# Centring the first two token tiles ahead of their roots in a gated two-layer kernel

## The chip, the core and the metric

The kernel runs on one NeuronCore of a Trainium2 chip. The metric is the device time of one execution in microseconds (us): the median of three runs, and beside it one execution under the hardware profiler, from which the rows come. TensorE multiplies matrices, VectorE and ScalarE work element by element, GpSimd issues the gathers and scatters of rows, SyncE (SP) issues the plain transfers.

## The reference

There are 2048 tokens of width 512. Two layers follow one another, each added to its input through a gate:

```
x = x + tanh(g_xattn) * experts_by_token_id(layernorm(x))     # 4 experts
x = x + tanh(g_ffn) * (top-2 of 16 experts + shared MLP)(layernorm(x))
```

In the first layer expert `e` uses one 512x512 matrix, its context `C`, for all three products: `y = (silu(h C^T) * (h C^T)) C^T`, where `h` is the normalised token `(x - mean) / sqrt(var + 1e-5)` and the expert follows from the token's id (ids of 18750 and more all go to the last of the four). The second layer routes each token to two of sixteen small gated MLPs, 256 places each, and adds a shared MLP. The change lies in the first layer alone.

## The kernel before

**Precision.** Products run in TensorE's fp32r form on operands split in two: a high part (the value rounded) and a low part (what is left). A product of two split operands is three matmuls: high by high, high by low, low by high (`product`, L1291). For a context the high part is a ScalarE copy (`high_ctx`, L562). The low part comes in one of two ways: VectorE subtracts (`low_ctx`, L834), or TensorE forms `ctx - high` with the identity and its negative (`rest`, L1320 and L1321) and ScalarE copies it out of PSUM (`take_rest`, L571).

**The opening.** VectorE sorts the tokens by expert into tiles of 128 rows, 19 places for tiles in all. GpSimd gathers the rows of the tiles (`gather_xa`, L433). SP loads the four contexts of 1 MB; the last of them goes out when the rows of tile 2 have landed, and four writes of zeros to spare rows of the output (256 KB each) follow it. The input gives tile 0 to expert 0, tile 1 to expert 1, tiles 2 and 3 to expert 2, the rest to expert 3. TensorE may begin the product of a tile of expert `w` once `ctx_lo_done` is above `w`.

**Stage 1.** Each engine runs its own `step(t)` for t from -2 to 20, and the order within a step is written out by hand. In step `t` the engines work on several tiles at once:

- for tile t+2: VectorE takes statistics (`bn_stats` L943, `bn_aggr` L961) and finds one over the root with ten small instructions on a column per tile (L976 to L993; "root" below); ScalarE applies scale and bias (`norm`, L583) into `h`;
- for tile t+1: TensorE transposes `h` (L1296), ScalarE copies the high part (`hT`, L608), VectorE subtracts for the low part (`low_h`, L925);
- for tile t: TensorE forms the product with the context into `psG`, ScalarE takes silu (L605), VectorE multiplies (`gate1`, L932) into `gu`;
- for tile t-1: TensorE transposes `gu`, high and low parts follow (L589, `low_g` L921), and the second product goes into `psY`;
- for tile t-2: VectorE adds the result to x (L916), takes statistics (L950) and the root together with tile t+2; ScalarE normalises for the second layer (L583), SP writes these rows to `padded` (L380) and GpSimd scatters x and h to the output buffer (L445).

The buffers of `h`, `hT`, `gT`, `gu` and `psY` are few, so the steps are tied by semaphores. VectorE, ScalarE and TensorE take their instructions strictly in program order. In ScalarE's step 1 the high part of context 3 stands ahead of silu:

```
if known == 1:
    high_ctx(3)
...
if have(known, 0):
    act.wait_ge(p_ps, t + 1)
    ...
    act.activation(s_sb[:, 0:D], psG[0][:, :], ACT.Silu).then_inc(s_ready, 1)
```

In the opening of before, tile 0 has its own root; tiles 1 and 2 share one ("pair"). Context 1's low part is one VectorE pass of 2048 columns, context 2's comes from four `rest` products, context 3's from two VectorE passes of 1024 columns in steps 1 and 2. SP's loop over tiles also sends the slices of the shared MLP's weights: two of 192 KB for each of the tiles 1 to 4, one for each of the tiles 5 to 8.

Of the kernel before, what the change touches and what calls it, by code (L numbers as in the profile page):

```python
# [31 lines left out]
P = 128  # L32
# [46 lines left out]
def gated_layer(nc, x, ids, ctx_t, gates, w13, w2, gate_b, const, out):  # L79
    stack = ExitStack()  # L80
    with stack:  # L81
# [91 lines left out]
        stats = sb("stats", [P, 2, 6])  # L173
        mv = sb("mv", [P, 2, 2])
        nwt = sb("nwt", [P, 5, 2])
# [57 lines left out]
        ctx_hi_done, ctx_lo_done = sem("ctx_hi_done"), sem("ctx_lo_done")  # L233
# [95 lines left out]

        def ctx_raw(e):  # L330
# [23 lines left out]
        def _(sp):  # L354
# [20 lines left out]
            sp.wait_ge(zeroed, 1)  # L375
            for a, b in ((a, b) for a in range(NA) for b in range(2)):
                sp.dma_start(out[TOK + a * P:TOK + (a + 1) * P, b * D:(b + 1) * D], zeros[:, :]).then_inc(spare_sent, 16)
            for t in range(NT):
# [5 lines left out]
                if 1 <= t <= 4:  # L384

                    for n in range(2):
                        load_slice((t - 1) // 2, 2 * ((t - 1) % 2) + n)
                elif 5 <= t <= 8:

                    load_slice(2, t - 5)  # L390

# [22 lines left out]
        def _(pool):  # L414
# [133 lines left out]
        def _(act):  # L548
# [15 lines left out]
            def take_rest(e, i):  # L564

                act.wait_ge(rest_ps, e // 2 * KD + i + 1)
                if e and i == KD - 1:

                    act.wait_ge(ctx_lo_done, 2)
# [8 lines left out]
            high_ctx(2)  # L578
# [7 lines left out]
            def step(t, par, known):  # L586
# [14 lines left out]
                if have(known, 0):  # L601
# [3 lines left out]
                    act.activation(s_sb[:, 0:D], psG[0][:, :], ACT.Silu).then_inc(s_ready, 1)  # L605
# [8 lines left out]
                act.wait_ge(norm_ready, t + 3)  # L614
                if have(known, 2):
                    if had(known, 1):
                        act.wait_ge(hT_ps, t + 1)
                    norm(h[:, par, :], xa_of(t, par, known), 1 if known == 0 else 0, h_ready)
                if known == FIRST:
                    take_rest(2, 0)  # L620
# [180 lines left out]
        def _(dve):  # L801
# [76 lines left out]
            for j in range(NJ):  # L878
# [17 lines left out]
                                     ALU.is_ge, ALU.add).then_inc(tile_ready, 1)  # L896
            dve.wait_ge(tg_ready, 1)
# [10 lines left out]
            def step(t, par, known):  # L908
                one, two = have(known, 2) and known != 0, have(known, -2)
# [18 lines left out]
                def gate1():  # L928
# [3 lines left out]
                    dve.tensor_tensor(gu[:, 0:D], s_sb[:, 0:D], psG[0][:, :], ALU.mult).then_inc(gu_ready, 1)  # L932

                if known == 0:
                    gate1()
                    low_h()

                pair = known == FIRST + 1
                cs = slice(0 if one else 1, 2 if two or pair else 1)
# [4 lines left out]
                low_g()  # L944
                if pair:
                    xa_landed(dve, 0, 0, 0)
                    i = dve.bn_stats(stats[:, 1, :], xa_of(0, 0, 0))
# [3 lines left out]
                k = t + 2  # L951
                if one or two:
# [4 lines left out]
                if one or two:  # L957
                    dve.wait_ge(stats_done, NORMS(k, known))
# [3 lines left out]
                    if two or pair:  # L962
                        i = dve.bn_aggr(mv[:, 1, :], stats[:, 1, :])
                    i.then_inc(mv_done, 1)
                    dve.wait_ge(mv_done, NORMS(k, known))
                    base = (NORMS(k, known) - 1) * NEWTON
# [12 lines left out]
                    for m in range(2):  # L979
                        nw(dve.tensor_tensor(T, V, Y, ALU.mult))  # L980
                        nw(dve.tensor_tensor(T, T, Y, ALU.mult))
                        if m == 0:
                            nw(dve.scalar_tensor_tensor(Y, T, -((27 / 4 * RS_W) ** (1 / 3)), Y, ALU.add, ALU.mult))
                            if pair:
                                low_h()
                    nw(dve.scalar_tensor_tensor(T, T, -10 / 3 * RS_W, T, ALU.add, ALU.mult))
                    if had(known, 2):
                        dve.wait_ge(h_ready, t + 2)
# [652 lines left out]
```

## Time and profile before

| quantity | value |
|---|---|
| median of 3 runs | 479.32 us (479.09 to 480.01) |
| profiled execution | 480.27 us, of which the span of instructions is 478.5 us |
| TensorE busy | 460.1 us, 96% of the span |
| VectorE busy | 328.6 us, 69% |
| ScalarE busy | 255.4 us, 53% |
| GpSimd busy | 211.1 us, 44% |
| mean granted clock of TensorE | 0.995 |

TensorE's share is an average over the whole run. In the first 5 us it does nothing; from 10 us on it is busy nearly throughout. Stage 1 ends near 160 us; behind it come the second layer's shared MLP, the routing and the sixteen experts.

### The profile page before, as it was taken

How to read it: one execution, taken by the hardware profiler on the slowest of the kernel's cores; microseconds unless marked ns; L12 is line 12 of the kernel's file. 1: busy time of each engine (PE TensorE's matmuls, PEld its weight loads, DVE VectorE, ACT ScalarE, POOL GpSimd, SP SyncE). 2: the span in 40 equal slices, each digit the busy share in tenths (PEclk: the TensorE clock that was granted, in tenths of full speed). 3: DMA queues.
4: the chain of work that ended last, by engine and by line, in shares of the span. 5: the costliest groups of instructions: out<-in, count | busy, mean ns of one | idle time of the engine just before them, and what ended most of it. 6: DMA issues, size and time to landing. Idle time of an engine off the chain costs nothing.

```text
span 478.5 us, 7813 instructions
## 1 busy us (share of the span) xinstructions
PE 460.1 (96%) x2493; PEld 392.7 (82%) x2493; DVE 328.6 (69%) x724; ACT 255.4 (53%) x379; POOL 211.1 (44%) x175
## 2 busy tenths in 40 slices
PE   2999999999999999999999999999999999999993
PEld 1477778888888888888888999999999999999992
DVE  6689899998987844488559776676666666667520
ACT  4764445545553543542436575656655676666531
POOL 0513444565443475435177445434525545542242
PEclk9999999999999999999999999999999999999998
DMA  7643656876665443363379999989869998887555
GB/s 298 187 174 125 198 179 201 292 258 226 206 214 175 175 121 114 86 79 46 43 198 185 296 294 264 267 279 272 266 193 263 254 267 269 264 248 226 110 63 70
DMA packets 30460, 95.02 MB, mean 199 GB/s; under 512 B 4960, under 2 KB 7008, under 8 KB 29920
## 3 DMA queue, kind: packets, MB, share of 16 engines
q0 software_dynamic: 17040, 43.66, 37.3%
q1 hardware_dynamic: 13104, 50.98, 31.2%
q8 instruction: 17, 0.28, 0.2%
q14 instruction: 11, 0.09, 0.1%
q10 hardware_dynamic: 288, 0.01, 0.0%
HBM read 67.50 MB, written 28.70 MB: 201 GB/s over the span
## 4 chain that ended last, share of the span: by engine, by line
PE 91%; DVE 3%; DMA 2%; ACT 1%; issue 1%; POOL 0%; POOLq 0%; DVEq 0%
PE psG L1291 49%; PE psY L1291 30%; PE psT L1296 7%; PE psG L1549 1%; DMA out<-xh_sb,idx 1%; PE psG L1320 1%; DMA tok_i<-in_ids 1%; PE psY L1308 1%; ACT arena L571 0%; POOLq L81 0%; ACT arena L562 0%; PE psY L1427 0%; PE psG L1321 0%; POOL out L521 0%; ACT front L583 0%
## 5 line engine op out<-in xcount | busy, mean ns | idle before, releaser
L1291 PE MATMUL psY<-arena 128*128 (+1 forms) x372 | 91.0, 394 | 0.4 <-DVE arena L921 0.4
L1291 PEld LDWEIGHTS psY<-arena 128*128 128x128 f32 x372 | 68.8, 188 | 14.8 <-issue 0.8
L512 POOL DMA_INDIRECT ht<-out,idx x32 | 33.6, 1051 | 64.6 <-PE psT L1296 48.8
L1291 PE MATMUL psY<-slot,arena 128*128 128x512 f32 x240 | 59.0, 395 | 0.0
L1066 DVE TENSOR_TENSOR slot<-raw,slot 128x1536 fp32r<-128x1536 f32 x25 | 43.9, 1760 | 19.7 <-ACT slot L638 19.6
L1291 PE MATMUL psG<-arena 128*128 x228 | 57.0, 398 | 0.0
L1066 DVE TENSOR_TENSOR arena<-raw,arena 128x1536 fp32r<-128x1536 f32 x24 | 42.0, 1756 | 16.6 <-ACT arena L638 16.4
L1291 PEld LDWEIGHTS psY<-slot,arena 128*128 128x128 f32 x240 | 44.2, 188 | 9.5 <-ACT xh_sb L682 0.3
L1291 PE MATMUL psG<-arena,slot 128*128 128x512 f32 x216 | 51.3, 392 | 0.0
L1291 PEld LDWEIGHTS psG<-arena 128*128 128x128 f32 x228 | 41.5, 188 | 8.5 <-issue 0.4
L1291 PEld LDWEIGHTS psG<-arena,slot 128*128 128x128 f32 x216 | 40.1, 188 | 8.2
L753 ACT ACTIVATE s_sb<-psG 128x224 f32<-128x224 f32 (+1 forms) x48 | 17.5, 365 | 54.8 <-PE psG L1291 54.8
L521 POOL DMA_INDIRECT out<-ys,idx x16 | 31.7, 1980 | 31.2 <-ACT ys L742 22.4
L521 POOL DMA_INDIRECT out<-xb,idx x16 | 29.7, 1853 | 33.3 <-ACT xb L742 23.1
L1291 PE MATMUL psG<-bl,slot 128*128 128x256 f32 (+1 forms) x264 | 42.1, 314 | 0.0
L1291 PE MATMUL psG<-slot,bl 128*128 128x448 f32 x192 | 40.3, 365 | 0.0
L1291 PE MATMUL psG<-arena,bl 128*128 128x448 f32 x192 | 40.3, 365 | 0.0
L1291 PEld LDWEIGHTS psG<-bl,slot 128*128 128x128 f32 x264 | 37.3, 189 | 3.0
L433 POOL DMA_INDIRECT front<-in_x,idx x17 | 17.0, 999 | 51.3 <-ACT front L583 39.9
L498 POOL DMA_INDIRECT out<-xh_sb,idxc x16 | 27.8, 1738 | 26.5 <-ACT xh_sb L682 24.6
L1291 PEld LDWEIGHTS psG<-slot,bl 128*128 128x128 f32 x192 | 36.0, 188 | 3.4
L1291 PEld LDWEIGHTS psG<-arena,bl 128*128 128x128 f32 x192 | 36.0, 188 | 3.3
(228 smaller groups left out, 803.9 us busy)
## 6 DMA issues: line engine op xcount, KB each, us to landing
raw<-in_w SPq DMA_DIRECT2D x48, 768.0 KB, 5.6
padded<-xh_sb SPq DMA_DIRECT2D x19, 256.0 KB, 2.2
raw<-in_w SPq DMA_DIRECT2D x12, 192.0 KB, 4.3
raw<-in_ctx_t SPq DMA_DIRECT2D x2, 1024.0 KB, 8.7
ht<-in_ctx_t SPq DMA_DIRECT2D x1, 1024.0 KB, 11.7
xh_sb<-in_ctx_t SPq DMA_DIRECT2D x1, 1024.0 KB, 9.5
out<-log_sb SPq DMA_DIRECT2D x4, 256.0 KB, 8.2
ht<-out,idx POOLq DMA_INDIRECT x32, 4.5
```

Of the source, the lines that this page charges most:

```text
L433: pool.indirect_dma_start(buf, None, x, rows_of(t, 0)).then_inc(xa_here[t if t < 4 else t % 2], 16)
L498: pool.indirect_dma_start(halves_of_out, ranked(1, j), y2[j % 4], None, compute_op=ALU.add).then_inc(y2_sent[j % 4], 16)
L512: pool.indirect_dma_start(ht[:, n, :], None, halves_of_out, slots(e * NA + a, 0)).then_inc(g_here[n], 16)
L521: pool.indirect_dma_start(halves_of_out, slots(e * NA + a, 1), y3[e % 2][:, a, :], None, compute_op=ALU.add).then_inc(added[a], 16)
L753: act.activation(dst, src, ACT.Silu).then_inc(silu3, 1)
L1066: dve.tensor_tensor(piece(SLOT[r][1], c), raw[:, c, :], as_f32(piece(SLOT[r][0], c)), ALU.subtract).then_inc(w_lo[c], 1)
L1291: ins = pe.matmul(ps, left[a], right[b], start=n == 0 and m == 0, stop=n == total - 1 and m == 2)
L1296: ins = pe.transpose(ps[:, k * P:(k + 1) * P], src[:, k * P:(k + 1) * P], ident)
L1308: ins = pe.matmul(psY[1][:, 0:2 * NT], onehot1[:, j, :], q_tok[0][:, j, 0:2 * NT], start=j == 0, stop=j == NJ - 1)
L1320: pe.matmul(psG[i][:, :], ident, ctx_raw(e)[:, s], start=True, stop=False)
L1549: ins = pe.transpose(psG[3][:, o:o + P], gu[:, s:s + P], ident)
```

## The change

Tiles 0 and 1 are no longer normalised before their first product, only centred: VectorE subtracts the mean of tile 0, ScalarE that of tile 1. The factor one over the root is applied behind the product, as the scale of silu and as a factor in the gate. One root then serves tiles 0, 1 and 2. Context 1's low part is half a VectorE pass (after GpSimd's first two gathers, `first_out`) and half two `rest` products; context 2's is two VectorE passes, in steps 0 and 1. In step 1 VectorE does the gate and the low part of h before the next tile's statistics and root. Tile 0's first product runs in three passes, one for each pair of parts, with a wait ahead of each. The zeros of the spare rows are written behind tiles 9 to 12. The core of the diff:

```diff
 SP
-            sp.wait_ge(zeroed, 1)
-            for a, b in ((a, b) for a in range(NA) for b in range(2)):
-                sp.dma_start(out[TOK + a * P:..., b * D:(b + 1) * D], zeros[:, :])...
             for t in range(NT):
...
+                elif 9 <= t <= 12:
+                    if t == 9:
+                        sp.wait_ge(zeroed, 1)
+                    a, b = divmod(t - 9, 2)
+                    sp.dma_start(out[TOK + a * P:..., b * D:(b + 1) * D], zeros[:, :])...
 GpSimd
             gather_xa(0)
+            gather_xa(1)
             pool.memset(cur[:, :], 0).then_inc(first_out, 1)
-            for t in range(1, 4):
+            for t in range(2, 4):
                 gather_xa(t)
 ScalarE
             take_rest(0, 0)
             take_rest(0, 1)
-            high_ctx(2)
             take_rest(0, 2)
             take_rest(0, 3)
...
+                    if known in CENTERED:                      # CENTERED = (0, 1)
+                        act.wait_ge(norm_ready, 1)
+                        act.activation(s_sb[:, 0:D], psG[0][:, :], ACT.Silu,
+                                       scale=nwt[:, 3, known:known + 1]).then_inc(s_ready, 1)
...
                 if known == -1:
-                    take_rest(2, 1)
-                    take_rest(2, 2)
+                    act.wait_ge(mean1_ready, 1)
+                    act.activation(h[:, 1, :], xa[:, 1, :], ACT.Identity, bias=nwt[:, 4, 1:2]).then_inc(h_ready, 1)
+                    take_rest(1, 2)
+                    high_ctx(2)
                 if known == 0:
-                    take_rest(2, 3)
+                    take_rest(1, 3)
...
-                if known == FIRST:
-                    take_rest(2, 0)
 VectorE
+            dve.wait_ge(first_out, 1)
+            low_ctx(1, 0, 2).then_inc(ctx1_half, 1)
...
+                    if known in CENTERED:
+                        dve.scalar_tensor_tensor(gu[:, 0:D], psG[0][:, :], nwt[:, 3, known:known + 1], s_sb[:, 0:D],
+                                                 ALU.mult, ALU.mult).then_inc(gu_ready, 1)
...
+                if known == FIRST:
+                    mean_of(0)
+                    dve.tensor_scalar(h[:, 0, :], xa[:, 0, :], mv[:, 0, 0:1], None, ALU.subtract).then_inc(h_ready, 1)
+                    mean_of(1)
+                    dve.tensor_scalar(nwt[:, 4, 1:2], mv[:, 1, 0:1], -1.0, None, ALU.mult).then_inc(mean1_ready, 1)
                 if known == 0:
                     gate1()
                     low_h()
+                    link(low_ctx(2, 0, 2))
+                if known == 1:
+                    low_g()
+                    dve.wait_ge(ctx_lo_done, 2)
+                    low_ctx(2, 1, 2).then_inc(ctx_lo_done, 1)
+                    gate1()
+                    low_h()
...
+                third = known == FIRST + 1
+                if third:
+                    low_h()
+                cs = slice(0 if one or third else 1, 3 if third else 2 if two else 1)
...
-                if have(known, 0) and known != 0:
+                if have(known, 0) and known > 1:
                     gate1()
-                if have(known, 1) and known not in (FIRST + 1, 0):
+                if have(known, 1) and known > 1:
                     low_h()
-                if pair:
-                    dve.wait_ge(ctx_lo_done, 1)
-                    low_ctx(1, 0, 1).then_inc(ctx_lo_done, 1)
 TensorE
             for i in range(KD):
                 rest(0, i)
-            rest(2, 0)
-            pe.wait_ge(rest_taken, KD)
+            pe.wait_ge(rest_taken, 1)
...
+                if known == 0:
+                    for m, (a, b) in enumerate(((0, 0), (0, 1), (1, 0))):
+                        pe.wait_ge(*((hT_hi, 1), (ctx_lo_done, 1), (hT_lo, 1))[m])
+                        for k in range(KD):
+                            ins = pe.matmul(psG[0][:, :], hT[a][:, k * P:(k + 1) * P], ctx(0, k)[b],
+                                            start=m == 0 and k == 0, stop=m == 2 and k == KD - 1)
+                    ins.then_inc(p_ps, 1)
...
                 if known == -1:
-                    rest(2, 1)
-                    rest(2, 2)
+                    rest(1, 2)
                 if known == 0:
-                    rest(2, 3)
+                    rest(1, 3)
```

`mean_of(k)` waits for the rows of tile k and takes `bn_stats` and `bn_aggr` of them, with its own waits on VectorE between the two.

## Rows read from the trace of the kernel before

**Rows 1.** The chain that ended last, opening and stage 1 (start us, us, what).

```profile
20.80 0.63 PE psT L1296 x4
...
49.37 6.94 DMA out<-xh_sb,idx
...
62.46 1.23 PE psT L1296 x8
```

**Rows 2.** TensorE's waits, whole run (us in total, times, longest us).

```profile
PE psT L1296 <- DVE gu L932: 1.1, 2, 0.8
```

**Rows 3.** Timeline of VectorE (start us, us; idle before and releaser in brackets).

```profile
16.16 0.69 DVE L943 BATCH_NORM_STATS2 stats<-front 128x6 f32<-128x512 f32 x1 [2.65 <-DMA front<-in_x,idx]
...
17.17 0.15 DVE L976 TENSOR_SCALAR nwt<-mv 128x1 f32<-128x1 f32 x1
...
23.72 2.29 DVE L834 TENSOR_TENSOR arena<-raw,arena 128x2048 fp32r<-128x2048 f32 x1
...
29.75 0.69 DVE L921 TENSOR_TENSOR arena<-psT,arena 128x512 fp32r<-128x512 f32 x1 [0.83 <-ACT arena L589]
...
30.57 0.15 DVE L976 TENSOR_SCALAR nwt<-mv 128x1 f32<-128x1 f32 x1
...
32.38 0.69 DVE L932 TENSOR_TENSOR gu<-s_sb,psG 128x512 f32<-128x512 f32 x1
32.99 0.68 DVE L925 TENSOR_TENSOR arena<-psT,arena 128x512 fp32r<-128x512 f32 x1
33.59 1.21 DVE L834 TENSOR_TENSOR arena<-xh_sb,arena 128x1024 fp32r<-128x1024 f32 x1
34.84 0.75 DVE L916 SCALAR_TENSOR_TENSOR xh_sb<-psY,tg,xb 128x512 f32<-128x512 f32 x1
35.50 0.68 DVE L943 BATCH_NORM_STATS2 stats<-front 128x6 f32<-128x512 f32 x1
...
40.83 1.25 DVE L834 TENSOR_TENSOR arena<-xh_sb,arena 128x1024 fp32r<-128x1024 f32 x1
...
56.51 0.75 DVE L916 SCALAR_TENSOR_TENSOR xh_sb<-psY,tg,xb 128x512 f32<-128x512 f32 x1 [1.15 <-DMA out<-xh_sb,idx]
```

**Rows 4.** Timeline of GpSimd, the opening.

```profile
15.19 0.95 POOL L433 DMA_INDIRECT ys<-in_x,idx  x1 [0.30 <-issue]
...
25.20 1.62 POOL L433 DMA_INDIRECT front<-in_x,idx  x1 [3.83 <-ACT front L583]
...
40.82 0.94 POOL L433 DMA_INDIRECT front<-in_x,idx  x1 [4.02 <-ACT front L583]
```

**Rows 5.** Timeline of ScalarE, the opening.

```profile
19.34 0.82 ACT L583 ACTIVATE front<-front,nwt 128x512 f32<-128x512 f32 x1
...
29.61 1.91 ACT L562 ACTIVATE arena<-xh_sb 128x2048 fp32r<-128x2048 f32 x1
31.49 0.60 ACT L605 ACTIVATE s_sb<-psG 128x512 f32<-128x512 f32 x1
```

**Rows 6.** Timeline of TensorE, the opening.

```profile
17.86 0.79 PE L1321 MATMUL psG<-arena,minus 128*128 128x512 f32 x1
...
22.35 1.02 PE L1320 MATMUL psG<-ht,cst 128*128 128x512 f32 x2
...
23.44 2.93 PE L1291 MATMUL psG<-arena 128*128 x12
...
28.46 2.99 PE L1291 MATMUL psG<-arena 128*128 x12
```

**Rows 7.** Timeline of SP's queue, the opening (start us, us of issue).

```profile
18.95 0.33 SPq L373 DMA_DIRECT2D xh_sb<-in_ctx_t  x1
```

**Rows 8.** DMA issues of 18.85 to 20 us (KB each, us from issue to landing).

```profile
xh_sb<-in_ctx_t SPq DMA_DIRECT2D x1, 1024.0 KB, 9.5
```

**Rows 9.** DMA packets by size, of 22 to 23 us and of 27 to 28 us.

```profile
DMA packets 33, 0.26 MB, mean 262 GB/s; under 512 B 1, under 2 KB 1, under 8 KB 1
...
DMA packets 204, 0.39 MB, mean 391 GB/s; under 512 B 34, under 2 KB 34, under 8 KB 201
```

More of the change, by code:

```diff
@@ L390, in _ @@
                     load_slice(2, t - 5)
+                elif 9 <= t <= 12:
+                    if t == 9:
+                        sp.wait_ge(zeroed, 1)
+                    a, b = divmod(t - 9, 2)
+                    sp.dma_start(out[TOK + a * P:TOK + (a + 1) * P, b * D:(b + 1) * D], zeros[:, :]).then_inc(spare_sent, 16)
             sp.wait_ge(bT_ps, NJ)
@@ L908, in step @@
             def step(t, par, known):
-                one, two = have(known, 2) and known != 0, have(known, -2)
+                one, two = have(known, 2) and known > 0, have(known, -2)
                 if two:
@@ L950, in step @@
                     i = dve.bn_stats(stats[:, 1, :], xh_sb[:, par, 0:D])
-                k = t + 2
-                if one or two:
+                groups = t + 3 if known >= 1 else 3
+                base = NEWTON * max(t, 0)
+                if one or two or third:
                     i.then_inc(stats_done, 1)
@@ L956, in step @@
                     transposed(TB + 1)
-                if one or two:
-                    dve.wait_ge(stats_done, NORMS(k, known))
+                if one or two or third:
+                    dve.wait_ge(stats_done, groups)
                     dve.nop(nofuse=True)
@@ L961, in step @@
                         i = dve.bn_aggr(mv[:, 0, :], stats[:, 0, :])
-                    if two or pair:
+                    if two:
                         i = dve.bn_aggr(mv[:, 1, :], stats[:, 1, :])
+                    if third:
+                        i = dve.bn_aggr(mv[:, 2, :], stats[:, 2, :])
                     i.then_inc(mv_done, 1)
-                    dve.wait_ge(mv_done, NORMS(k, known))
-                    base = (NORMS(k, known) - 1) * NEWTON
+                    dve.wait_ge(mv_done, groups)
                     n = [0]
@@ L983, in step @@
                             nw(dve.scalar_tensor_tensor(Y, T, -((27 / 4 * RS_W) ** (1 / 3)), Y, ALU.add, ALU.mult))
-                            if pair:
-                                low_h()
                     nw(dve.scalar_tensor_tensor(T, T, -10 / 3 * RS_W, T, ALU.add, ALU.mult))
-                    if had(known, 2):
-                        dve.wait_ge(h_ready, t + 2)
+                    if third or one:
+                        dve.wait_ge(h_ready, t + 2 if one else 2)
                     if had(known, -2):
@@ L1058, in rank_tokens @@
                 dve.tensor_copy(idxc[:, 2, :], S(31)).then_inc(rank_idx, 1)
-            def NORMS(k, known):
-                return (1, 2, None, 3)[k] if known is not None and known < 2 else k
             def split(s, c, r):
@@ L1346, in step @@
             def step(t, par, known):
-                if have(known, 0):
+                if have(known, 0) and known > 0:
                     w = weights(t)
@@ L1365, in step @@
                     half_up(0, 1)
-                if have(known, 0):
+                if known == 0:
[5 more added lines that the diff above has]
+                    ins.then_inc(p_ps, 1)
+                elif have(known, 0):
                     pe.wait_ge(hT_lo, t + 1)
```

49 lines of the change are left out of this document (29 added, 20 removed).

## The prediction

> **What bounds the kernel now.** I read the chain that ended last first. In the opening it runs over all engines, and the first transposes of a token tile stand at 20.80 us; from 62.46 us on it is TensorE alone [rows 1]. So whatever the change wins must reach 62.46. Between the two the chain runs through VectorE and, at 49.37, through a 6.94 us scatter of finished rows. TensorE's waits say the same: for gates it waited twice, 1.1 us in all [rows 2]. So VectorE's timeline came next [rows 3]. From 29.75 us it works without a gap to 55.36, where it waits 1.15 for that scatter: statistics, the small root instructions, gate, low parts, in program order. The landmark is L916 at 34.84, which adds the first finished tile to x; I call it X0. From X0 to the scatter and on to 62.46 each step hangs on VectorE's order, which the change leaves alone there. A shift of X0 is therefore a shift of the end, one for one, and what TensorE wins in the opening counts only as far as X0 moves.
>
> **The parts, one by one.** Times are from the span's start; those for the changed kernel are my sums.
>
> *First tile.* VectorE now first takes half of context 1's low part, once GpSimd has issued two gathers. The third gather began at 15.19 [rows 4], so the half starts near 15.1; such a half takes 1.25 to the next instruction (33.59 to 34.84 [rows 3]). It ends at 16.35, close to the 16.16 of the first statistics before. From statistics to the next step but one is 1.01 (16.16 to 17.17). The subtraction of the mean over 128x512 is not in the trace: it is bounded by a one-column instruction, 0.15 (L976), and ScalarE's scaled copy of the same tile, 0.82 [rows 5]. The nearest row is a VectorE pass over 512 columns, 0.60 from start to start (32.99 to 33.59). The tile is then ready near 18.0, at the latest 18.2. TensorE ends its four residual products of context 0 at 18.65 (17.86 plus 0.79 [rows 6]), which covers both bounds. The transposes run from 18.65 to 19.28 (0.63 [rows 1]), 2.15 earlier than before.
>
> *First product.* One residual of context 1 (1.09, 22.35 to 23.44 [rows 6]) lies between, so the product starts near 20.2 and, at 2.93, ends at 23.1 in place of 26.37: 3.2 won on TensorE. Its three passes are still twelve matmuls, at no cost; the low part of h, wanted by the third, is there at 20.6.
>
> *The root moves behind the product.* VectorE reaches the statistics of tile 2 only after that low part, near 20.6. Then 1.01, the root 1.81 (30.57 to 32.38 [rows 3]) and 0.1 to ScalarE: the first silu starts at 23.6, not 23.1. Silu now reads its scale from a column. That form is not in the trace; 0.60 (L605, no column) and 0.82 (L583, two) bound it [rows 5], and I add 0.1. Tile 1's mean is taken no later than tile 2's rows, whose landing released SP at 18.95 [rows 7]; its copy, one evacuation and the high part of context 2 (0.82, 0.60, 1.91) end by 23.5 at worst, under that wait.
>
> *Second product.* It needs context 1 whole. ScalarE does silu, a copy of h and the last residual first, three times 0.6 with a little overlap: 25.3. The gate's transposes take 0.6, so the product starts near 26.0 and ends at 29.0 (2.99), against 31.45 before. Here 2.4 are still won.
>
> *Where it is lost again.* In the step of tile 1 gate and low part of h now stand ahead of tile 3's statistics and root; before, root and statistics ran while VectorE waited for silu anyway. From the start of that silu to X0 it was 31.49 to 34.84, 3.35. Now it is silu 0.70, gate as a three-operand instruction 0.66 (34.84 to 35.50), low part 0.60, statistics 1.01, root 1.81, half of context 3 1.25: 6.03. With silu at 29.0, X0 is at 35.0, 0.2 later than before. This is the floor of the sum. Context 2's first half costs nothing more: it stands where the whole of context 1 stood (2.29 at 23.72 [rows 3]), and the second half fits before silu, from 27.2 to 28.5.
>
> *Context 3 decides above the floor.* On ScalarE the high part of context 3 stands ahead of that silu, in both kernels. Before, it ran at 29.61 for 1.91 and silu followed at 31.49 [rows 5], so the load, issued at 18.95 and landed 9.5 later at 28.45 [rows 7, 8], cost nothing. Now silu could start at 29.0, so the load must have landed by 27.1; otherwise X0 is the landing plus 1.91 plus 6.03. A landing at 28.45 gives 36.4, 1.6 late.
>
> *Does the load come earlier?* The four writes of zeros, 1 MB, no longer follow it. But from 22 to 23 us 32 of 33 packets were of 8 KB or more, the load's, and from 27 to 28 still 3 of 204 [rows 9]: while it was fast it was nearly alone, and its last pieces came late, a few at a time. At 32 packets each us its 128 would take 4 us and, with 2 us before the first, land at 25: the low bound. I let the 9.5 stand, because the zeros were issued after the load, and because the gathers of tiles 4 and 5 now go out earlier (their buffers come free near 18.0 and 20.6) and mix with its last pieces. The Trainium skill, "DMA: Bandwidth & Descriptors", section "Queues, rings and completion order", says that each engine takes one ring's descriptors in order. By it zeros queued behind the load don't hold it up, and the landing stays at 28.45 or later; by equal sharing it would come near 26, and X0 at the floor. No row separates the two fully.
>
> *Is the load issued later?* SP waits for tile 2's rows. That gather began at 15.19, and now the half context is running on VectorE by then. A gather begun at 25.20, within such a subtraction (23.72 plus 2.29), took 1.62 and ended 0.81 after it; one begun at 40.82, just ahead of the subtraction at 40.83, took 0.94 [rows 3, 4]. The new one comes second, so I expect it held until 16.35: 1.0. Bounds 0 and 1.2. The load is then issued near 19.95 and lands at 29.45: X0 at 37.4, 2.6 late.
>
> *The rest.* Zeros at tiles 9 to 12 are 256 KB each on SP's queue behind the padded rows, with nothing close behind; tiles 5 to 8 have weight slices of 192 KB in that place. TensorE alone is on the chain there. I put it at nothing, at most 0.3.
>
> **Sum.** Floor 0.2; with the load at 28.45, 1.6; with the held gather, 2.6. I take the middle of the last two, 2.1. The profiled execution took 480.27 (span 478.5) and would take 482.4. It lies 0.95 above the median of the three runs, 479.32; on that median the forecast is 481.4. About 0.2%, 0.96 us, is what a measurement can tell from no change.
>
> **Rivals.** (1) The load lands by 27.8, since the zeros did share its engines after all. For it: packets of other transfers were the most by 27 us, while its last pieces came. Against: by 23 us none of them had moved and the late pieces stayed late. X0 is then 0.2 to 0.9 late, 479.5 to 480.2: no measurable change. (2) Faster: X0 at 33.9 or before decides, so silu of tile 1 at 27.8 or before. ScalarE would have to finish context 1 at 24.1 and so start the first silu at 22.4, an us before the root can end. If the 2.4 won at the second product came through, it would be 476.9. The sequence of waits speaks against it. (3) The gathers of tiles 4 and 5 alternate with the load's last pieces, and it lands at 30 or later: X0 3.1 late or more, 482.5 upward. (4) The opening does not open earlier: tile 0 is held by something I don't see, its transposes stay at 20.8. Silu of tile 1 is then at 31.15 and X0 at 37.2, 2.3 late: 481.7, since tile 1's step is reordered anyway. The mean needs no root, so this is unlikely.
>
> **How the numbers follow.** Forecast (load lands 27.9 to 29.9, X0 1.0 to 3.0 late): 0.53. Rival 1: 0.27. Rival 2: 0.12. Rivals 3 and 4: 0.05 and 0.03. Slower by over 0.2% is 0.61, within it 0.27, faster 0.12. The range runs from the good end of rival 1, less some 0.5 of error in my waits, 479.0, to the start of rival 3, 482.7; the forecast's own is 480.3 to 482.3.
>
> **What would show it.** First transposes near 18.7; the first silu released by the root, near 23.6; the second product near 26.0; the high part of context 3 waiting for the load, which lands at 28 or later; tile 1's silu right behind it; VectorE idle ahead of that gate by one to two us; X0 at 36 to 37.5; the last wait for a gate near 64 to 65 in place of 62.46. A third gather of about 1.9 us shows the held issue; 0.95 shows it wrong. A landing at or under 27 makes the forecast wrong towards no change; X0 under 34 makes it wrong altogether.

## The result and the profile after

Measured side by side, the changed kernel took 481.60 us (median of 12 runs, 479.17 to 482.72) and the kernel before 479.38 (12 runs, 478.66 to 480.99). The ratio is 1.0033, 95% interval 1.0019 to 1.0048: slower, by 0.9 to 2.3 us. The forecast was 481.4 and "slower". The time was right; the cause I gave for it was not. The profiled execution took 481.71 with a span of 479.6, the one of before 480.27 and 478.5; TensorE's mean granted clock was 0.997 and 0.995, so the clock is not the difference.

The opening first. TensorE's timeline of the changed kernel (start us, us, what; idle before and its releaser in brackets), the rows that answer to [rows 6] and the first of [rows 1]:

```profile
18.08 0.60 PE L1329 MATMUL psT<-cst,front 128*128 128x128 f32 x4
...
19.61 2.88 PE L1403 MATMUL psG<-arena 128*128 128x512 f32 x12
...
25.34 3.01 PE L1324 MATMUL psG<-arena 128*128 x12
```

ScalarE's timeline of the changed kernel, against [rows 5]:

```profile
23.13 0.69 ACT L612 ACTIVATE s_sb<-psG,nwt 128x512 f32<-128x512 f32 x1 [0.86 <-DVE nwt L1033]
...
26.04 1.91 ACT L568 ACTIVATE arena<-xh_sb 128x2048 fp32r<-128x2048 f32 x1
...
28.39 0.69 ACT L612 ACTIVATE s_sb<-psG,nwt 128x512 f32<-128x512 f32 x1 [0.45 <-PE psG L1324]
```

GpSimd's timeline, SP's timeline and, from the DMA issues, the landing of the load of context 3 in the changed kernel, against [rows 4, 7, 8]:

```profile
15.09 1.90 POOL L438 DMA_INDIRECT ys<-in_x,idx  x1 [0.18 <-issue]
```

```profile
19.34 0.33 SPq L376 DMA_DIRECT2D xh_sb<-in_ctx_t  x1
```

```profile
xh_sb<-in_ctx_t SPq DMA_DIRECT2D x1, 1024.0 KB, 6.4
```

The opening went as worked out, with one exception, the load. First transposes, first product and second product come some 0.6 us earlier than forecast, and the first silu is released by the root. The third gather is held for 1.90. The load is issued only 0.39 later than before (19.34 against 18.95), where I had 1.0. And it lands 6.4 us after its issue, at 25.72, not at 28.45 or later. The high part of context 3 starts at 26.04 without a wait, and the silu of tile 1 waits for TensorE's product alone.

VectorE's timeline of the changed kernel, the tiles' x1 (L928, which was L916), against [rows 3]:

```profile
34.45 0.75 DVE L928 SCALAR_TENSOR_TENSOR xh_sb<-psY,tg,xb 128x512 f32<-128x512 f32 x1
...
54.90 0.74 DVE L928 SCALAR_TENSOR_TENSOR xh_sb<-psY,tg,xb 128x512 f32<-128x512 f32 x1
...
76.08 0.75 DVE L928 SCALAR_TENSOR_TENSOR xh_sb<-psY,tg,xb 128x512 f32<-128x512 f32 x1 [1.61 <-DMA out<-xh_sb,idx]
...
129.91 0.75 DVE L928 SCALAR_TENSOR_TENSOR xh_sb<-psY,tg,xb 128x512 f32<-128x512 f32 x1 [0.95 <-DMA out<-xh_sb,idx]
...
157.20 0.74 DVE L928 SCALAR_TENSOR_TENSOR xh_sb<-psY,tg,xb 128x512 f32<-128x512 f32 x1
```

The x1 of tiles 6 and 18 in the kernel before, on VectorE:

```profile
76.38 0.75 DVE L916 SCALAR_TENSOR_TENSOR xh_sb<-psY,tg,xb 128x512 f32<-128x512 f32 x1
...
156.98 0.74 DVE L916 SCALAR_TENSOR_TENSOR xh_sb<-psY,tg,xb 128x512 f32<-128x512 f32 x1
```

X0 is 34.45, 0.39 earlier than before. At 54.90 (x1 of tile 3) the lead is 1.61, since before waited 1.15 for a scatter there [rows 3]. At 76.08 (x1 of tile 6) it is down to 0.30: now this x1 waits 1.61 for the scatter of tile 4, whose buffer it needs. At 129.91 (x1 of tile 14) another 0.95 goes to the scatter of tile 12. The chain that ended last of the changed kernel names the same two, and after stage 1 a gather that TensorE waits 0.4 for:

```profile
68.65 7.23 DMA out<-xh_sb,idx
...
122.75 6.96 DMA out<-xh_sb,idx
...
162.75 1.98 DMA padded<-xh_sb
164.86 4.46 DMA front<-padded,idxc
```

TensorE's share of the chain is down to 75% from 91%. So the loss is not in the opening. It is at waits for scatters, 40 and 95 us later, and 0.4 at that gather. How much the scatters cost isn't read from these two executions alone: the one of before had a scatter wait itself and lay 0.9 over its median, so that the last x1 differs by 0.22 only (156.98 and 157.20). A repeat of the kernel before, further down, had no such wait and its last x1 at 156.13, 1.07 ahead of the changed one.

The time from X0 to the last x1, taken over all fourteen profiled executions of this document, tells what the waits cost. Where no x1 waited for a scatter (six executions) it was 120.7 to 121.0 us. Where x1 of tile 3 or of tile 6 waited (seven) it was 122.1 to 123.7, 122.75 in the changed kernel. So of the changed kernel's 1.8 over 121.0 the wait at tile 6 is the greater part: two kernels that have it and none at tile 14 (zeros in the opening, zeros at tile 0, both below) took 122.3 and 122.7, so the wait at tile 14 adds at most 0.4, not its 0.95. Where no scatter is late, x1 waits for TensorE's product at tiles 11 to 16, 1.6 us in all, and a wait for a scatter takes the place of part of that. From the last x1 to the end of the span it was 321.4 to 322.6 in all fourteen.

The trace's landing events of the scatter issued at 68.65 say more: fifteen of its sixteen parts had landed after 5.46 us, the last after 7.23. Near 71.8 a single packet of 16 KB of the instruction queue stands among the others. DMA packets of the changed kernel from 71.5 to 72.5 us (queue, packets, MB, share of 16 engines):

```profile
q1 hardware_dynamic: 158, 0.22, 58.2%
q0 software_dynamic: 48, 0.17, 41.1%
q8 instruction: 1, 0.02, 6.0%
```

In the kernel before the corresponding one stands at 68.8, before the scatter of tile 4 is issued at 70.62 (68.4 to 69.4 us):

```profile
q0 software_dynamic: 48, 0.14, 35.5%
q8 instruction: 1, 0.02, 6.5%
```

The queue carried 17 such packets in either run. TensorE's built program has 5,375 instructions in the kernel before and 5,325 in the changed one, by far the most of the engines, so I take the packets to be TensorE's.

The Trainium skill, "Runtime: NRT & Kernel Launch", section "Instruction fetch mechanics", says that an engine refills its instructions by a DMA queue of its own, in blocks of 16 KiB (256 instructions), and calls the cost mostly hidden. The packet size agrees; whether the cost is hidden is what follows.

### The profile page after: what moved, and what is told of

The parts are those of the page before. It is cut to its first block, busy times and chain, and to the rows that moved or that the text cites. A ratio compares the mean times of both kernels' runs of the same rounds, so it can differ in the third digit from the quotient of the medians.

```text
span 479.6 us, 7779 instructions
## 1 busy us (share of the span) xinstructions
PE 458.2 (96%) x2487; PEld 391.2 (82%) x2487; DVE 329.4 (69%) x718; ACT 253.7 (53%) x376; POOL 209.8 (44%) x175
## 4 chain that ended last, share of the span: by engine, by line
PE 75%; DVE 11%; DMA 7%; issue 2%; ACT 2%; POOL 1%; POOLq 0%; SPq 0%; DVEq 0%; ACTq 0%
PE psG L1324 42%; PE psY L1324 24%; PE psT L1329 5%; DMA out<-xh_sb,idx 3%; DMA raw<-in_ctx_t 2%; PE psG L1588 1%; DVE xh_sb L928 1%; DVE stats L990 1%; DMA out<-ys,idx 1%; PE psG L1353 1%; DVE stats L982 1%; DVE arena L933 1%; DMA front<-padded,idxc 1%; DVE nwt L1022 1%; DVE nwt L1023 1%
## 5 line engine op out<-in xcount | busy, mean ns | idle before, releaser
L1324 PE MATMUL psG<-arena 128*128 x216 | 54.1, 399 | 0.0
L1324 PEld LDWEIGHTS psG<-arena 128*128 128x128 f32 x216 | 39.2, 188 | 7.7
L527 POOL DMA_INDIRECT out<-xb,idx x16 | 28.6, 1786 | 35.0 <-ACT xb L752 15.8
L648 ACT ACTIVATE slot<-raw 128x1536 fp32r<-128x1536 f32 x25 | 37.0, 1484 | 0.9 <-DMA raw<-in_w 0.9
```

What stands on the lines that cost most here:

```text
L527: pool.indirect_dma_start(halves_of_out, slots(e * NA + a, 1), y3[e % 2][:, a, :], None, compute_op=ALU.add).then_inc(added[a], 16)
L648: act.activation(piece(SLOT[r][0], c), raw[:, c, :], ACT.Copy).then_inc(w_hi[c], 1)
L1324: ins = pe.matmul(ps, left[a], right[b], start=n == 0 and m == 0, stop=n == total - 1 and m == 2)
```

## The experiments

**A**, the recorded theory: the opening sets X0, and X0's shift is the shift of the end. **B**: the zeros, in their new place, lengthen the scatters of tiles 9 to 12 until x1 waits for them. **C**: the end is set by scatters that land about 7 us after their issue, because a block of TensorE's instructions is fetched through the same DMA engines meanwhile; whatever the opening wins is given back at that wait. Each kernel below was timed in 11 or 12 runs beside 35 of the kernel before, whose medians were 479.40 (first four), 479.64 (next four) and 479.74 (last four). The expectations name the wait for the scatter of tile 12 sometimes by the scatter's tile and sometimes by x1's, tile 14; it is the same wait.

**Zeros in the opening again.** The change without its last part:

```diff
             sp.dma_start(bias_b[:, :], gate_b).then_inc(in_bias, 16)
+            sp.wait_ge(zeroed, 1)
+            for a, b in ((a, b) for a in range(NA) for b in range(2)):
+                sp.dma_start(out[TOK + a * P:TOK + (a + 1) * P, b * D:(b + 1) * D], zeros[:, :]).then_inc(spare_sent, 16)
...
-                elif 9 <= t <= 12:
-                    if t == 9:
-                        sp.wait_ge(zeroed, 1)
-                    a, b = divmod(t - 9, 2)
-                    sp.dma_start(out[TOK + a * P:TOK + (a + 1) * P, b * D:(b + 1) * D], zeros[:, :]).then_inc(spare_sent, 16)
```

> The changed kernel with the zeros written in the opening again, right behind the load of context 3 and the bias; tiles 9 to 12 write none. Theory A (the opening alone sets the end): the load lands later than the 6.4 us it now takes, 8 to 9.5, X0 moves from 34.45 to 36 or 37 and the end with it, so 1.5 to 2.5 us over the changed kernel, about 483.5. Theory B (the zeros cost where they now stand): the wait of 0.95 at x1 of tile 12 is gone and the time is 0.6 to 1.0 under the changed kernel, about 480.8. Theory C (what the opening wins or loses is given back at the first scatter that lands late, and that is set by a fetch of TensorE's instructions): the end stays within 1 us of the changed kernel's, whatever X0 does, and a scatter of about 7 us stands on the chain wherever it waits.

480.90 (479.30 to 482.18), ratio 1.0023 [1.0011, 1.0036]. ScalarE of this kernel:

```profile
26.98 1.92 ACT L566 ACTIVATE arena<-xh_sb 128x2048 fp32r<-128x2048 f32 x1 [0.35 <-DMA xh_sb<-in_ctx_t]
```

VectorE of this kernel:

```profile
76.64 0.75 DVE L926 SCALAR_TENSOR_TENSOR xh_sb<-psY,tg,xb 128x512 f32<-128x512 f32 x1 [1.61 <-DMA out<-xh_sb,idx]
```

With the zeros behind it the load landed in 7.3 us; its high part waited 0.35 and X0 was 34.95. So A's 483.5 falls: even then no 2 us are lost at the load. (The landing of 8 to 9.5 us that A set out from did not come either.) The wait at tile 14 is gone, as B said; the 1.61 at tile 6 stays, as C said.

**Zeros late, nothing else changed.** The kernel before with the zeros at tiles 9 to 12, the two hunks above the other way round:

> The kernel before with one part of the change alone: the zeros are written at tiles 9 to 12. Theory A: context 3 was not waited for before, so no change, 0.0 with 0.4 either way. Theory B: slower by 0.6 to 1.0 us, with a wait of about 1 us for a scatter at tiles 11 to 13 that the kernel before doesn't have. Theory C: scatters 9 to 12 take some 1 us longer, but a wait shows only where an instruction fetch falls into the same scatter, so between 0 and 1.0. The load of context 3 should land 6 to 7 us after its issue in place of 9.5 if the zeros were what held it.

480.18 (479.37 to 481.63), 1.0013 [1.0001, 1.0025]. VectorE of this kernel:

```profile
108.37 0.75 DVE L918 SCALAR_TENSOR_TENSOR xh_sb<-psY,tg,xb 128x512 f32<-128x512 f32 x1 [1.44 <-DMA out<-xh_sb,idx]
```

So x1 of tile 11 waits for the scatter of tile 9, which took 6.3 us, as B said. But C is in it too: fifteen of that scatter's parts had landed after 5.14 us and the last 1.13 later, with a packet of the instruction queue 2.7 us behind the issue. And the wait left nothing behind: from X0 to the last x1 this execution took 121.0 us, as those without a wait. So the 0.0013 of the ratio, whose interval nearly reaches no change, isn't explained by it. The load of context 3 took 8.8 here, though no zeros stood behind it, so these weren't what held it in this execution:

```profile
xh_sb<-in_ctx_t SPq DMA_DIRECT2D x1, 1024.0 KB, 8.8
```

**Zeros behind tile 0's padded rows**, the rest as changed:

```diff
                 sp.dma_start(padded[t * P:(t + 1) * P, :], xh_sb[:, t % 2, D:2 * D]).then_inc(padded_sent[t % 2], 16)
+                if t == 0:
+                    sp.wait_ge(zeroed, 1)
+                    for a, b in ((a, b) for a in range(NA) for b in range(2)):
+                        sp.dma_start(out[TOK + a * P:TOK + (a + 1) * P, b * D:(b + 1) * D], zeros[:, :]).then_inc(spare_sent, 16)
...
-                elif 9 <= t <= 12:
...
```

> The changed kernel with all four writes of zeros behind the padded rows of tile 0 (near 37 us, before the first scatter is issued) in place of tiles 9 to 12. Theory A: no change against the changed kernel, 481.6. Theory B: 0.6 to 1.0 faster than that, 480.8, since nothing is added to the scatters of tiles 9 to 12. Theory C: the wait at tile 12 goes (0.95) but the one at tile 4 (1.61) stays, 480.6 to 481.2; if the zeros delay the padded rows or the first scatter, up to 0.5 is lost again.

480.50 (478.87 to 481.72), 1.0016 [1.0004, 1.0028]; a wait of 1.67 at tile 6, 0.17 at tile 9 and none at tile 14. B's and C's waits as expected.

**Tile 1's order put back.** In VectorE's step of tile 1 `gate1()` and `low_h()` stand behind statistics and root again, as in every later tile:

```diff
                     low_ctx(2, 1, 2).then_inc(ctx_lo_done, 1)
-                    gate1()
-                    low_h()
...
-                if have(known, 0) and known > 1:
+                if have(known, 0) and known >= 1:
                     gate1()
```

> The changed kernel with the step of tile 1 in the order of before: statistics and root ahead of the gate and the low part of h. Theory A: VectorE was idle 0.92 us ahead of that gate, so X0 comes up to 0.9 earlier, 33.6, and the end too: 480.7. Theory C: X0 comes 0.5 to 0.9 earlier, but the end doesn't follow: the gain is taken by the scatter of tile 4, whose wait grows by the same amount, so within 0.5 of the changed kernel, 481.6, unless the shift moves the fetch out of that scatter, and then 1.6 faster.

479.54, but from 477.29 to 482.28; 0.9998 [0.9982, 1.0015]. X0 was 33.81. The median is under both A's 480.7 and C's 481.6, and nearest to the 480.0 that C had for a fetch moved out of the scatter. The profiled execution, at 481.59 one of the long ones, waited 4.5 us for scatters in three places (VectorE, x1 of tiles 6, 11 and 14):

```profile
75.31 0.75 DVE L928 SCALAR_TENSOR_TENSOR xh_sb<-psY,tg,xb 128x512 f32<-128x512 f32 x1 [1.43 <-DMA out<-xh_sb,idx]
...
109.23 0.75 DVE L928 SCALAR_TENSOR_TENSOR xh_sb<-psY,tg,xb 128x512 f32<-128x512 f32 x1 [1.83 <-DMA out<-xh_sb,idx]
...
130.28 0.75 DVE L928 SCALAR_TENSOR_TENSOR xh_sb<-psY,tg,xb 128x512 f32<-128x512 f32 x1 [1.21 <-DMA out<-xh_sb,idx]
```

Up to tile 6 X0's gain of 0.64 is still there (0.77 against the changed kernel); at tiles 11 and 14 it is lost. That it reaches the end in the short runs is likely, but none of them has a trace.

**A third buffer for finished rows** in the changed kernel, in columns idle in stage 1, with semaphores for each of the three:

```diff
+        XH = [xh_sb[:, 0, :], xh_sb[:, 1, :], big_all[:, NJ * P // 2:NJ * P // 2 + 2 * D]]
...
-                    if known is None or known >= 4:
-                        dve.wait_ge(xh_sent[par], landed(t - 4, par))
+                    if known >= 5:
+                        dve.wait_ge(xh_sent[(t - 5) % 3], 16 * ((t - 5) // 3 + 1))
```

> The changed kernel with a third buffer for finished rows (in columns that are idle in stage 1), so that x1 of a tile waits for the scatter of three tiles back, not two. Theory C (the opening's gain is given back at a scatter that lands about 7 us after its issue): no wait for a scatter is left, the 1.6 at tile 6 and the 1.0 at tile 14 go, and the time falls by 1.5 to 2.5 against the changed kernel, to 478.6 to 479.6; X0 stays near 34.5. Theory A (the opening itself is the loss, X0's shift being the end's): the scatters are no bound, so within 0.5 of the changed kernel's 481.1 to 481.6. Theory B (zeros at tiles 9 to 12): only the wait at tile 14 goes, 0.6 to 1.0 faster.

480.09 (479.40 to 480.36), 1.0006 [0.9997, 1.0016]. VectorE of this kernel, x1 of tiles 0, 6 and 18:

```profile
34.77 0.75 DVE L931 SCALAR_TENSOR_TENSOR xh_sb<-psY,tg,xb 128x512 f32<-128x512 f32 x1
...
74.79 0.75 DVE L931 SCALAR_TENSOR_TENSOR xh_sb<-psY,tg,xb 128x512 f32<-128x512 f32 x1
...
155.69 0.75 DVE L931 SCALAR_TENSOR_TENSOR xh_sb<-psY,tg,xb 128x512 f32<-128x512 f32 x1
```

No x1 waits for a scatter any more, x1 of tile 6 is 1.29 earlier than in the changed kernel, and the runs now lie within 1.0 us of each other, not 3.6. The time fell by 1.5 against 481.60, as C said, but 480.09 is over the 478.6 to 479.6 that C gave. Against the repeat of the changed kernel that ran beside this one (below) the median fell by 0.3 only, but no run is over 480.4, where 6 of 12 were. A had no change. Held against the repeat, the medians alone would not tell A from C; the vanished waits and the spread do.

**The same buffer in the kernel before:**

> The kernel before with the same third buffer. Theory C: its wait of 1.15 at tile 3 goes, 478.3 to 479.0, and it stands 0.2 to 0.8 behind the changed kernel with three buffers, by the 0.4 that X0 is later: the change itself would then be worth a small gain. Theory A: the kernel before stays ahead of the changed one by 1.5 with three buffers as with two.

479.24 (478.89 to 480.88), 0.9999 [0.9990, 1.0008]: little gained, and instead of standing 0.2 to 0.8 behind the changed kernel with three buffers it stands 0.85 ahead by the medians. VectorE of this kernel, x1 of tiles 0 and 18:

```profile
34.84 0.75 DVE L919 SCALAR_TENSOR_TENSOR xh_sb<-psY,tg,xb 128x512 f32<-128x512 f32 x1
...
155.62 0.75 DVE L919 SCALAR_TENSOR_TENSOR xh_sb<-psY,tg,xb 128x512 f32<-128x512 f32 x1
```

With scatters out of the way both kernels leave stage 1 at the same time, to 0.07 us in these two executions. What is left between 1.0006 and 0.9999 is within both intervals. The profile puts 0.46 of it at one gather after stage 1, for which TensorE waited in the changed kernel:

```profile
167.94 0.66 PE L1335 MATMUL psT<-cst,front 128*128 128x128 f32 x4 [0.46 <-DMA front<-padded,idxc]
```

That wait isn't the change's: the kernel before had it in the repeat below, with 0.6.

**Moving the fetch, first try:** empty instructions in TensorE's program, 72 in the changed kernel and 189, in two places, in the kernel before.

```diff
+            for _ in range(72):
+                pe.nop(nofuse=True)
             pe.wait_ge(digits_ready, 1)
```

> The changed kernel with 72 empty instructions at the head of TensorE's program, where it waits from 0 to 5.4 us anyway; nothing else. They move each later block of TensorE's instructions some 5 us earlier against the work. Theory C: the fetch at 71.8, 3.2 after the issue of the scatter of tile 4, falls ahead of that scatter or behind its rows, so the wait of 1.6 at tile 6 goes (another may come where a fetch falls 2 to 3.5 us behind an issue): 479.0 to 480.5. Theory A and theory B: 72 empty instructions under a wait change nothing, 481.1 to 481.6.

> The kernel before with 189 empty instructions in TensorE's program, 110 before its first wait and 79 before its second, both idle. They move its instruction blocks by about three quarters of a block, so that one falls near 72, as in the changed kernel. Theory C: the scatter of tile 4 lands 7 us after its issue, x1 of tile 6 waits 1 to 1.6 for it, and the time is 480.3 to 481.5 without any edit to the work. Theory A and theory B: no change, 479.4.

Neither tests anything: the built programs hold none of the empties, they are instruction for instruction those of the two kernels. As repeats they are of use. The changed kernel gave 480.39 (478.66 to 483.30), 1.0019 [1.0001, 1.0037]; the kernel before 479.71 (478.63 to 480.31). So over 24 runs the changed kernel spreads across 4.6 us, 9 of them under 480 and 11 over 481, and its price is 0.9 or 1.6 by the one ratio or the other. The load of context 3, whose 9.5 us [rows 8] the prediction let stand, took this in the repeat of the kernel before:

```profile
xh_sb<-in_ctx_t SPq DMA_DIRECT2D x1, 1024.0 KB, 7.5
```

And the x1 of its last tile, on VectorE, to be held against the changed kernel's 157.20:

```profile
156.13 0.74 DVE L916 SCALAR_TENSOR_TENSOR xh_sb<-psY,tg,xb 128x512 f32<-128x512 f32 x1
```

**Moving the fetch, second try:** by what the change itself took out of TensorE's program, the register reads of a tile's context. Put back in the changed kernel, and taken out of the kernel before:

```diff
                 if known == 0:
+                    w = weights(0)
...
-                                            hT[a][:, k * P:(k + 1) * P], ctx(0, k)[b],
+                                            hT[a][:, k * P:(k + 1) * P], ctx(w, k)[b],
```

```diff
-                if have(known, 0):
+                if known == 0:
+                    w = 0
+                    pe.wait_ge(ctx_lo_done, 1)
+                elif have(known, 0):
                     w = weights(t)
...
-                        ins = product(psY[0][:, :], [gT[0][:, s], gT[1][:, s]], ctx(v, k), k, KD)
+                        ins = product(psY[0][:, :], [gT[0][:, s], gT[1][:, s]], ctx(0 if known == 1 and k == 3 else v, k), k, KD)
```

> The changed kernel with one thing of the kernel before put back: tile 0's product again finds its context by a register read from the tile table, as every other tile does, not by a fixed address. The matmuls are the same; TensorE's built program grows from 5,325 to 5,363 instructions (5,375 in the kernel before), and each later block of it is fetched some 2 to 3 us earlier against the work. Theory C (scatter of tile 4 hit by the fetch near 72): the fetch comes near 69, less than an us after that scatter's issue, the scatter lands within 5.8, no wait at tile 6, 1.0 to 1.6 faster than the changed kernel, 479.2 to 480.0. Theory A and theory B: a register more under other waits changes nothing, 480.8 to 481.6.

> The reverse: the kernel before with a fixed address in tile 0's first product and in one of four pieces of its second. TensorE's built program shrinks from 5,375 to 5,328 instructions, three more than in the changed kernel; the opening and the zeros are those of before. Theory C: the fetch near 68 moves to 71 or 72, into the scatter of tile 4, which then lands 7 us after its issue; x1 of tile 6 waits 1 to 1.6 and the time is 480.3 to 481.2. Theory A and theory B: no change, 479.5.

The changed kernel with the registers: 480.22 (478.55 to 482.54), 1.0010 [0.9993, 1.0027]. The profiled execution had the packet at 72.1 all the same, and this on VectorE:

```profile
76.32 0.75 DVE L928 SCALAR_TENSOR_TENSOR xh_sb<-psY,tg,xb 128x512 f32<-128x512 f32 x1 [1.48 <-DMA out<-xh_sb,idx]
```

The kernel before without them: 480.26 (479.58 to 480.79), 1.0006 [0.9995, 1.0017]. Its packet came at 70.8, later as expected but only 1.3 us behind the scatter's issue; the scatter took 5.6, and no x1 waited. Both misses: 480.22 is over the 480.0 that C allowed (and under the 480.8 of A and B), and 480.26 came without the wait that C had for it. The length of TensorE's program alone doesn't place the fetch, and C's way to it is not shown by an edit. What is shown is how the two go together. The scatter of tile 4, in each profiled execution with two buffers (us; the packet's place from the packet records):

| kernel | issued | packet, behind issue | landed after | x1 of tile 6 waited |
|---|---|---|---|---|
| before | 70.62 | -1.8 | 5.2 | 0 |
| zeros late | 69.22 | -1.8 | 5.5 | 0 |
| repeat of before | 69.72 | -1.5 | 5.3 | 0 |
| before, no registers | 69.56 | +1.3 | 5.6 | 0 |
| order, registers, zeros (below) | 68.75 | +1.2 | 5.6 | 0 |
| changed | 68.65 | +3.2 | 7.2 | 1.61 |
| zeros in the opening | 69.19 | +3.5 | 7.2 | 1.61 |
| zeros at tile 0 | 69.03 | +3.4 | 7.3 | 1.67 |
| tile 1's order | 68.06 | +3.1 | 7.1 | 1.43 |
| repeat of changed | 68.46 | +3.1 | 7.2 | 1.56 |
| changed, registers | 69.00 | +3.1 | 7.1 | 1.48 |

Six of six with the packet 3.1 to 3.5 us behind the issue landed late, none of the five others did. The kernels with three buffers fit in: +2.7 and 6.8 us (nothing waits for it), +1.3 and 5.6, -1.7 and 5.3.

All scatters of stage 1 together say more: 266 in the fourteen executions. In 43 the last part came over 0.8 us behind the fifteenth, and in all 43 a packet of the instruction queue began between issue and landing. In 173 no packet did, and their last part was at most 0.7 behind. The reverse does not hold: 50 scatters had a packet in that time and no such late part.

The wait does not swallow the opening's gain, as C has it; it comes on top. From X0 to x1 of tile 6 the six with the late scatter took 41.5 to 41.8 us, with X0 anywhere from 33.81 to 34.95; the seven executions without a wait by then took 40.0 to 40.4.

The zeros show as clearly. In the five executions that write them at tiles 9 to 12, the scatters of tiles 9 to 11 took 5.3 to 6.7 us, and each had a wait of 0.9 to 1.8 at tile 11 or 14 or both. In the six others with two buffers those scatters took 3.7 to 4.8, and there was none at these tiles. The zeros don't do it alone, though. The wait at tile 14 is for the scatter of tile 12, and in all four executions that have it that scatter had a late part: in the changed kernel fifteen parts had landed after 5.58 us, the last after 6.96, and x1 could have started 6.21 behind the issue.

**Two versions from these.** The third buffer with tile 1's order put back, the two diffs above together:

> The changed kernel with the third buffer for finished rows and with tile 1's statistics and root ahead of its gate: two edits that each helped. Theory C: no wait for a scatter, X0 at 33.8, so 0.4 to 1.0 under the three buffers alone (479.9 mean): 478.9 to 479.5. Theory A: the earlier X0 comes through whole and alone: 479.2. Rival to both: TensorE, which already makes VectorE wait from tile 11 on with three buffers, takes up the earlier start: 479.9, no gain.

478.68 (477.82 to 479.57), 0.9979 [0.9966, 0.9991]: faster than both kernels, by 0.4 to 1.6 us against the one before. VectorE, x1 of tiles 0, 6 and 18:

```profile
33.22 0.75 DVE L931 SCALAR_TENSOR_TENSOR xh_sb<-psY,tg,xb 128x512 f32<-128x512 f32 x1
...
73.24 0.75 DVE L931 SCALAR_TENSOR_TENSOR xh_sb<-psY,tg,xb 128x512 f32<-128x512 f32 x1
...
154.17 0.75 DVE L931 SCALAR_TENSOR_TENSOR xh_sb<-psY,tg,xb 128x512 f32<-128x512 f32 x1
```

Against the third buffer alone X0 is 1.55 earlier and the last x1 1.52: the opening's gain arrives whole at the end of stage 1, and in the medians nearly so (1.4). In these two executions the spans differ by 0.7 only, since the part behind the last x1 took 0.8 longer. The rival, that TensorE takes up the gain, is wrong for stage 1. That X0 came 0.6 before the 33.8 expected is not the reordering alone: with the same order and two buffers X0 was 33.81 above and 34.45 below.

With two buffers, tile 1's order, the registers and the zeros at tile 0:

> The changed kernel with two buffers as it is, but with tile 1's statistics and root ahead of its gate, the register address of tile 0 back, and the zeros behind the padded rows of tile 0. Theory C: no fetch falls into the scatter of tile 4 and nothing lengthens those of tiles 9 to 12, so X0's 33.8 comes through to TensorE's own order: 478.3 to 479.0, under both kernels. Theory A: X0 0.6 earlier than the changed kernel's: 480.4. Theory B: 480.2.

479.11 (477.67 to 481.09), 0.9985 [0.9969, 1.0001]. C had 478.3 to 479.0 and X0 at 33.8; X0 was 34.45. The profiled execution had no wait for a scatter; the spread of 3.4 us suggests that others had. Without the third buffer the gain seems to stay a matter of chance.

## Why the prediction was right in its number and wrong in its cause

**The opening's steps held.** Transposes at 18.65 were 18.08, the first silu at 23.6 was 23.13, the second product at 26.0 was 25.34. Each is 0.5 to 0.7 early, 0.4 of it because TensorE's residual products, on which I set the first transposes, were done sooner: the last began at 17.44, not at 17.86 [rows 6]. The held gather was 1.90 for "about 1.9", but of the 1.0 that I had the load issued later by it only 0.39 came. The reordered step of tile 1, from silu to X0, was 6.06 for 6.03.

**The step that failed first: "I let the 9.5 stand".** The load landed in 6.4, 0.7 behind the 25 that I had as its low bound, so X0 was 34.45, 0.55 below my floor of 35.0, and not 36.4 to 37.4. I read one landing as a property of the queue. The same program gave 9.5 and 7.5. By the rule of the Trainium skill that I cited ("DMA: Bandwidth & Descriptors", "Queues, rings and completion order") zeros queued behind it don't hold it up. The fourteen executions don't contradict that: sorted by the opening, the five with the opening of before took 7.1 to 9.5, and the one without zeros among them 8.8; the nine with the changed opening took 6.4 to 7.4, and the one with zeros among them 7.3. What in the opening does set the landing is open.

**The second: "a shift of X0 is a shift of the end, one for one".** X0's shift does go through (1.55 and 1.52, above), but it is not the only one. With two buffers a late scatter adds its own: in the profiled executions X0 moved by 0.39 to the good and the end by 1.1 to the bad. (Repeats put X0 at 34.21 and 35.15, so the 0.39 is itself one draw.) The sign was in [rows 1, 3]: a 6.94 us scatter and a 1.15 wait behind it. I took it as a fixed piece of the chain. It was one outcome of a tight race: x1 of tile 6 could start 5.8 us after the issue of the scatter that it needs (76.08 - 1.61 - 68.65), and that scatter takes 5.2 to 5.6 when all goes well.

**The third: zeros at tiles 9 to 12 "at nothing, at most 0.3".** I looked for what stands behind them on SP's queue, and not at the scatters that share the DMA engines. There they lengthen scatters from 3.7 to 4.8 us to 5.3 to 6.7, and 0.9 to 3.0 us of waits stand at tiles 11 and 14 in a profiled execution. What that costs is less and not settled: 0.6 by the ratio of the kernel with them alone (interval from 0.05 to 1.2), at most 0.4 in the changed kernel's profiled execution, nothing in that of the kernel with them alone.

Of the rivals, the first was right about the load, and X0 came out between its 35.0 and the second's 33.9; none had a scatter in it. The forecast of 481.4 met 481.6 by two waits of 1.61 and 0.95 for scatters, where it had X0 2.1 late at the load. That is luck, and the repeat's 480.39 lies 1.0 lower.

**What is shown and what isn't.** That waits for scatters are what the changed kernel loses by is shown by the third buffer: no such wait is left and the ratio is 1.0006, its interval under that of 1.0033; against the repeat's 1.0019 the intervals overlap, so the exact share stays open, as do the 0.0007 between the two kernels with three buffers. That the zeros lengthen scatters is shown by moving them; what this costs at the end is not. That the instruction fetch makes a scatter late is argued, not shown: from eleven of eleven executions of the table and from 43 of 43 late parts. No edit moved it at will, what places the fetch isn't settled, and neither is why 50 scatters with a packet landed on time.

## What to carry to other kernels

Where a buffer comes free by a transfer with a margin of a few tenths of a microsecond, an edit upstream or an added transfer can decide whether a wait falls there, and one profile shows one draw: count the margin before summing shifts, and give the buffer a third copy before tuning what feeds it. A landing time read from one execution is a sample, and a sum that hangs on it needs a second one. When runs of one program spread over several microseconds, compare the spread too: in the changed kernel it fell from 3.6 to 1.0 when the waits were taken away. And not every wait on a page is a loss: the 1.44 us of the kernel with the zeros alone cost nothing at the end of stage 1, because x1 would otherwise have waited some 1.1 us for TensorE at tiles 11 to 14 (so it did in the repeat of the kernel before).

## What the runs showed of the hardware

A 16 KB packet of the instruction queue, about 1 us on its engine, went with a scatter of tile 4 whose last of sixteen parts came 1.7 to 1.9 us behind the fifteenth; in all six cases it stood 3.1 to 3.5 us behind the issue, while other queues' packets were moving too (158 of 207 in the window above). At 1.2 to 1.3 us behind the issue it did this scatter no harm. That is no rule: scatters of tiles 12 and 15 with a packet 1.1 to 1.6 us behind the issue had a last part 1.0 to 1.9 us late. The distance isn't all: the late scatter of the kernel before [rows 1] had its packet 4.5 us behind the issue, and the scatters of tile 1 in the ten other executions of that table had theirs 4.5 to 5.0 behind and landed in 5.1 to 5.4. A load of 1 MB in the same program took 9.5 us in one execution and 7.5 in another. A gather that GpSimd issued 0.15 us into a VectorE subtraction (14.94 to 16.16 us in the changed kernel) took 1.90 us; in the kernel before the third gather took 0.95.
